# One GpSimd product per unit of four states in place of two

## The reference, cut to what matters

```python
def step(state, inp):
    x_t, dt_t, B_t, C_t = inp
    dA = jnp.exp(dt_t[:, :, None] * A[None])
    state = state * dA + (dt_t * x_t)[:, :, None] * B_t[:, None, :]
    y_t = jnp.einsum('bds,bs->bd', state, C_t)
    return (state, y_t)
```

## Time and profile before

| | |
|---|---|
| median of 3 executions | 5839.85 us (5838.22 to 5840.39) |
| profiled execution, its own time | 5846.96 us |
| its span | 5845.0 us |
| TensorE matmuls busy | 5374.8 us, 92% |
| GpSimd busy | 5097.9 us, 87% |
| VectorE busy | 4834.3 us, 83% |
| ScalarE busy | 4067.0 us, 70% |
| granted TensorE clock, mean | 0.974 of full speed |

### The profile page before, as it was taken

One profiled execution on the slowest core, in us unless ns is written; L12 is line 12 of the kernel. 1 busy time (PEld: TensorE's weight loads), 2 busy tenths in 40 slices (PEclk: granted clock), 3 DMA queues, 4 the chain that ended last, 5 costly groups with the idle time before them and its releaser, 6 DMA issues.

```text
span 5845.0 us, 206313 instructions
## 1 busy us (share of the span) xinstructions
PE 5374.8 (92%) x86664; PEld 3347.2 (57%) x86664; DVE 4834.3 (83%) x4323; ACT 4067.0 (70%) x6785; POOL 5097.9 (87%) x2326
## 2 busy tenths in 40 slices
PE   5798999989899998999989999898999989999887
PEld 2455656556565555655656565565655656565554
DVE  0689888888888888888888888888888888898996
ACT  3767676776767677676776777767676776866664
POOL 0689898998989889898898988989899898999996
PEclk9899999999999999999999999999999999999999
DMA  5465554656546565555656556555465655656553
GB/s 153 156 156 193 137 185 171 158 186 148 189 152 172 180 151 185 148 171 179 158 191 140 180 171 155 194 145 187 152 176 183 151 186 146 175 180 159 198 176 115
DMA packets 578961, 977.34 MB, mean 167 GB/s; under 512 B 294881, under 2 KB 328450, under 8 KB 510466
## 3 DMA queue, kind: packets, MB, share of 16 engines
q1 hardware_dynamic: 313858, 961.82, 53.1%
q10 hardware_dynamic: 264192, 2.11, 2.8%
HBM read 875.74 MB, written 88.08 MB: 165 GB/s over the span
## 4 chain that ended last, share of the span: by engine, by line
PE 41%; POOL 33%; issue 18%; DVE 3%; ACT 3%; DMA 2%; POOLq 0%; DVEq 0%; ACTq 0%; SPq 0%
POOL H L605 30%; PE pUB L690 14%; PE Y L716 13%; PE pP L645 4%; DVE H L570 3%; PE pP L638 2%; DMA Cb<-scratch_c 2%; PE pP L663 2%; PE pA L742 2%; PE pP L651 1%; POOL lnv L619 1%; ACT dA L434 1%; POOL dto L623 1%; PE pA L735 1%; PE pA L729 1%
## 5 line engine op out<-in xcount | busy, mean ns | idle before, releaser
L570 DVE TENSOR_TENSOR_SCAN H<-dA,pUB 128x512 f32<-128x512 f32 x4096 | 4697.0, 1203 | 791.4 <-PE pUB L690 733.0
L605 POOL TENSOR_TENSOR H<-H,Cb 128x1024 f32<-128x1024 f32 x2048 | 4811.1, 2390 | 512.6 <-DVE H L570 492.6
L434 ACT ACTIVATE dA<-DT,w_negA 128x512 f32<-128x512 f32 x4096 | 2615.4, 710 | 1130.3 <-DVE H L570 1126.4
L690 PEld LDWEIGHTS pUB<-Bd,UT 64*64 64x64 f32 x65536 | 1952.5, 135 | 1291.9 <-issue 1278.9
L690 PE MATMUL pUB<-Bd,UT 64*64 64x128 f32 x65536 | 2274.9, 275 | 298.7 <-DVE H L570 227.6
L716 PE MATMUL Y<-H,w_ident 64*64 64x512 f32 x16384 | 2018.9, 603 | 63.0 <-POOL H L605 60.7
L716 PEld LDWEIGHTS Y<-H,w_ident 64*64 64x64 f32 x16384 | 659.2, 136 | 650.1 <-issue 641.9
L434 ACT ACT_TABLE_LOAD x224 | 287.4, 1283 | 4.0
L638 PE MATMUL pP<-hT,w_Win 128*128 128x512 f32 x512 | 263.7, 639 | 16.0 <-ACT uto L422 12.7
L645 PE MATMUL pP<-xs,w_taps 128*128 128x512 f32 x512 | 252.9, 617 | 4.2 <-ACT xs L373 2.9
L651 PE MATMUL pP<-U,w_dt_w 128*128 128x512 f32 x512 | 252.7, 617 | 3.4 <-ACT zo L386 3.4
(11 more groups left out here) (85 smaller groups left out, 2308.0 us busy)
## 6 DMA issues: line engine op xcount, KB each, us to landing
Cb<-scratch_c SPq DMA_DIRECT2D x512, 1024.0 KB, 5.2
Bd<-scratch_diag SPq DMA_DIRECT2D x512, 512.0 KB, 4.0
scratch_diag<-H SPq DMA_DIRECT2D x16, 1024.0 KB, 17.8
scratch_z<-zo SPq DMA_DIRECT2D x64, 256.0 KB, 5.7
scratch_dt<-dto SPq DMA_DIRECT2D x64, 256.0 KB, 5.8
scratch_ut<-uto SPq DMA_DIRECT2D x64, 256.0 KB, 6.3
DT<-scratch_dt SPq DMA_DIRECT2D x64, 256.0 KB, 5.1
UT<-scratch_ut SPq DMA_DIRECT2D x64, 256.0 KB, 5.5
```

What stands on the lines that cost most here:

```text
L434: last = nc.scalar.activation(dA[:, n % DAR, j, :], DT[:, k, :], ACT.Exp, scale=c["negA"][:, k, GS * blk + j:GS * blk + j + 1])
L570: last = nc.vector.tensor_tensor_scan(H[:, n % HR, 2 * i + j, :], dA[:, n % DAR, 2 * i + j, :], pUB[:, i, :].rearrange("p (t s) -> p s t", ...
L605: nc.gpsimd.tensor_tensor(h[:, j:j + 2, :], h[:, j:j + 2, :], Cb[:, blk % 2, j:j + 2, :], ALU.mult).then_inc(times_c, 1)
L690: last = nc.tensor.matmul(out, UT[rows, k, j * P + h * HP:j * P + h * HP + HP], Bd[rows, blk % 2, i, j * P:(j + 1) * P].rearrange("p (t s) ...
```

## The change

GpSimd's product is made once per unit, over all four states, in place of once per half. It waits for both halves of the scans, and adds 2 to `times_c` when it is done. The sums' waits are unchanged in the text of the kernel; since the count now moves by whole units, part 0 of a pair's sums waits for the whole product of the odd unit.

```diff
--- before.py
+++ after.py
@@ -600,9 +600,8 @@
                     if scan:
                         if n % 2 == 0:
                             pool.wait_ge(c_in[blk % 2], at(16 * (b * NBLK + n // 4 + 1)))
-                        for j in range(0, GS, 2):
-                            pool.wait_ge(state_done, at(2 * (GN * b + n) + j // 2 + 1))
-                            nc.gpsimd.tensor_tensor(h[:, j:j + 2, :], h[:, j:j + 2, :], Cb[:, blk % 2, j:j + 2, :], ALU.mult).then_inc(times_c, 1)
+                        pool.wait_ge(state_done, at(2 * (GN * b + n) + 2))
+                        nc.gpsimd.tensor_tensor(h[:, :, :], h[:, :, :], Cb[:, blk % 2], ALU.mult).then_inc(times_c, 2)
                     if close and n in turns["norm c"]:
                         shift_of(nc, pool, flipc, normc[0], normc[3], normc[4], c_)
                     if ffn and n in turns["norm 1"]:
```

## The result

| | before | after |
|---|---|---|
| median, us | 5840.12 (4 runs) | 7361.98 (4 runs) |
| profiled execution: time, span, us | 5846.96, 5845.0 | 7360.06, 7358.1 |
| granted TensorE clock, mean | 0.974 | 0.907 |

The ratio is 1.2607, 95% interval [1.2585, 1.2628]: 26% slower, where 21.6% was forecast. 7362 us lies in the range (6680 to 7450).

What follows compares the result with a forecast made beforehand. No engine is full; the order of hand-overs bounds the kernel. Chain 6431 + outside scans 248 + turn of B 78 + loop's end 32 + softplus steps 30 + clock 288 = 7107, given as 7100 us; range 6680 to 7450.

Steps and rivals of the forecast that it cites:

- The wait: Sum 0, a pair's first sum on TensorE, waits for the odd unit's whole product: starts 4.81 us after its scans (head).
- tail: From sum 0's start to the end of the next odd unit's scans, a TensorE and VectorE chain without slack: 7.75 us.
- The clock: TensorE's pauses in quiet pairs lower its clock: 12 pairs a batch at 1.49 us, 288 us over 16 batches.
- the loop's end: TensorE idles between sum 0 and the next force, only issue to blame: 2.7 us for each of 12 turns, 32 us.
- the slow sum behind B: At the turn of B, two long pieces of TensorE work, sum 0 runs 3.59 us, not 1.90: 1.6 more.
- The other work: TensorE's work besides forces and sums fits busy pairs, leaving 1.2 us idle; only the turn of B costs, 78 us.
- The softplus work: GpSimd's three 1.27 us operations, four times a batch: hidden after an even unit, 0.5 us late after an odd one.
- The port: VectorE's L579 may wait up to 4.6 us for a long GpSimd product; charged 2 us a batch, 30 us.
- A: Rival: TensorE's clock holds despite the pauses, 6810 us; chance 0.20.
- B: Rival: TensorE's clock falls in busy pairs too, 7570 us; chance 0.12.
- C: Rival: faster, GpSimd is the bound and the long product saves 172 us of it, 5668 us; chance 0.03.
- D: Rival: no change, TensorE's other work covers the wait everywhere; chance 0.02.

Runs made afterwards that it cites:

- even_whole: Against the kernel before: one whole product for the even unit of each pair, two half products for the odd unit; 6116.89 us, ratio 1.0454.
- odd_whole: Against the kernel before: two half products for the even unit of each pair, one whole product for the odd unit; 7317.07 us, ratio 1.2495.
- after_force_first: Changed kernel with part 0 of a pair's sums moved on TensorE behind the next pair's first force; 6729.05 us, ratio 1.1463 to the kernel before.
- count_late: Kernel before, still two half products per unit, but times_c raised by 2 at the second one; 6280.5 us, ratio 1.0731.
- fill: Changed kernel with eight zero-adding matmuls ahead of part 0 of the sums, at 16 odd steps of a batch; 7016.25 us, ratio 1.1978.
- before_soft51: Kernel before with the last softplus step of VectorE and GpSimd moved from step 49 to 51; 5830.55 us, ratio 0.9939.

## Why the prediction was right, and where it was off

**The wait.** The step that carries the forecast held to a tenth of a microsecond: one product 4.53 us (4.58 forecast), sum 0 at +4.82 (4.81), tail 7.80 (7.75), busy period 12.62 (12.56). The start of the sum is as close as that by a little luck: the product started 0.14 us after the scans (0.08 forecast) and was 0.05 shorter. `even_whole` against `odd_whole` shows that it is the odd unit's product, and `after_force_first` that part of the loss is the force queued behind the waiting sum. `count_late` shows that the count by itself costs 7.3%; the rest comes with the odd unit's product being whole. In both kernels the product that raises the count starts after the last scan; the whole one lasts 2.2 us longer, and the usual head of a quiet pair went from 2.65 to 4.82 us.

**The clock.** The mechanism was right, and `fill` shows it; the term was mis-sized. Slow tails cost 263 x (9.79 - 7.80) = 524 us, where I had 288 for the clock, 32 for the loop's end and about 22 (14 x 1.6) for the slow sum behind B, 342 together. I charged 12 pauses in each of 16 batches, 192; there were 263 slow tails. In the loop's 13 batches the fourteen quiet pairs gave 159, 12.2 a batch, as charged. To these come 13 at the turn of B, and 22 in the softplus pairs, which pause too. The other three batches have 69 rather than 36: the last one, with little other work, 29 of 31, the first and the last but one 21 and 19. And a slow tail costs more than the 1.49 us read from the earlier trace rows. There the pause lay behind sum 0, and the low clock slowed a force and a part of sum 1; here the pause is ahead of sum 0, which alone takes 1.7 us more. The means hold more than the clock, too: behind the last pair of a batch the median tail is 13.0 us, with the idle time at the loop's end in it. The softening by "two in three of the pauses" was also wrong in the last seven pairs of a batch: in all pairs with steps 50 to 63 the tails were slow in 12 or 13 of the loop's 13 batches.

**The other work.** In busy pairs it fitted, as worked out: the median head is 4.81 to 4.83 us in 12 of the 13 pairs from step 4 to 29; the other is the turn of B, with 9.06 (8.8 forecast).

**The softplus work.** "After an even unit it is hidden" failed. The even unit's product starts late in a busy pair (its scans end late because of TensorE's other work), so 3.8 us behind it reach past the odd unit's scans: heads of 7.19 and 6.41 us. I had 30 us for all effects at these steps; the two heads alone are 14 x (2.4 + 1.6) = 56 us.

**The port.** L579 never had to wait for a long product to end: its maximum fell from 4.0 to 0.85 us, and the median is 0.67 (ns min/median/max):

```profile
L579 DVE SCALAR_TENSOR_TENSOR ev<-ev,absv x64: 665/667/853, 138.0 to 6741.1; 128x512 f32<-128x512 f32 x64
```

The rule of the Trainium skill that I weighed there ("GPSIMD Engine Reference", section "Specifications") thus costs at most 0.2 us a time in the changed kernel; the 5.2 us a step that I kept as an end never came.

**The sum.** Forecast 7107 for the profiled execution. Tails at full clock +0.05 x 512 = 26, slow tails 524 - 342 = +182, heads: (5.07 - 4.81) x 512 = 131 found, 56 for B and 30 for the rest forecast = +45. Together 7360, against 7360.06. That it meets to the microsecond is chance: 0.01 us in a mean is 5 us over 512 pairs.

**The rivals.** A (the clock holds) was wrong: 263 tails were slow. B (it falls in busy pairs too) was wrong in place: in the busy pairs between steps 4 and 29 the loop's batches have no slow tail outside the turn of B. In time the truth lay between the forecast and B. C and D failed on the wait: TensorE stood for the product in 497 pairs of 512.

**The range.** Its upper end, 7450 us, holds about three quarters of the 475 us that B adds to the forecast, not half as the prediction says. With half it would have ended near 7340 us, below the 7362 measured.

## What to carry to other kernels

When two instructions are merged, ask who waits for the first of them, and what stands in that engine's queue behind the waiting instruction: here 0.2 us saved per product cost 1 to 5 us a pair. Write the cycle of hand-overs for one period from a single timeline, and check that it gives the present period before changing a term in it. Where a new pause appears on TensorE, price the low clock behind it, count the pauses in every part of the run, and try a few matmuls that add zeros in the pause: work that does nothing was worth 5% here.

## What the runs showed of the hardware

- A product of 2048 columns on GpSimd takes 4.53 us, one of 1024 2.37: 2.16 us for 1024 columns and about 0.2 fixed. The Trainium skill, "GPSIMD Engine Reference", section "Elementwise — side-by-side cycle accounting", has 4497 ns for an add of that size; the product here is within 1% of it.
- Behind the waits the low clock follows the pause and not the wait: with pauses of about 3.5 us in the quiet pairs the mean granted clock was 0.907, and with the same heads but pauses under 2 us it was 0.968.
- A pause is not the only thing ahead of a low clock. At the turn of B in the kernel before it fell though TensorE had been busy for all of the 11 us from 2070 to 2081, and the sum behind it was slow. The next stretch (length, busy us of PE, PEld, DVE, ACT and POOL, clock, DMA share, GB/s):

```profile
2081.00:2091.00 10.00, 10.00 (x94) 7.79 (x98) 4.48 (x4) 1.99 (x4) 4.03 (x3) 0.54 0.30 107
```

- TensorE stands at times before a force with nothing but issue to blame (2.24 us inside one in `count_late`), and how much changes from version to version: 63.4 us in the kernel before, 96.2 in `count_late`, 50.3 in `before_soft51`, 28.9 in the changed kernel. No run here shows what sets it.
